# Projection stage of a two-layer graph network: query and key parts of four chunks per store, and value weights with the head index innermost

## The chip, the cores and the metric

The kernel runs on one core of a Trainium2 chip. The metric is the device time of one execution in microseconds (us); lower is better.

## The reference

A graph of 3327 nodes with 128 features, adjacency matrix `adj`, two layers. What matters here is layer 1:

```python
h = jnp.maximum(_layernorm(x), 0.0)
q = (h @ Wq.T).reshape(128, n, 8)      # 128 heads of the score matrix, 8 values for each node
k = (h @ Wk.T).reshape(128, n, 8)
v = (h @ Wv.T).reshape(128, n, 8)
a = softmax(einsum('dnh,dmh->dnm', q, k) * scale + adj + adj, axis=2)
x = x + einsum('dnm,dmh->dnh', a, v).reshape(n, 1024) @ Wo.T
```

The reshape is of memory as it lies, so one row of `h @ W.T` (1024 numbers for one node) is 128 groups t of 8 numbers h. The kernel calls t the token within a node and h the head index, and one scratch tensor in DRAM holds the 3328 x 128 = 425,984 tokens.

## The kernel before

The program is a row of stages, each closed by a barrier of all engines: a norm of the input, a stream over the adjacency matrix (layer 0), `finish_first_layer`, `project` (q, k and v of layer 1), `bound_scores`, a stage that is skipped when the bound is small, `split_shift`, the attention (by far the longest), and `project_out`. The change touches `finish_first_layer`, `project` and the scope of one tile.

**`finish_first_layer`** turns the weights on TensorE into PSUM (`y`), and ScalarE copies them to `w_t` (L432), columns in the order kind, h, t. ScalarE copies `wo_t` behind it (L433), and its next work is a square root (L435) that needs VectorE's variance.

**`project`** goes over C = 26 chunks. A chunk is 128 nodes, one for each partition (node p * 26 + c), so that each has a row of 1024 numbers for q, k and v. For each chunk:

- TensorE (L576) makes q, k, v in three PSUM tiles `pyq`, `pyk`, `pyv`, one of each, so the next chunk's q waits until VectorE and ScalarE have read this one's.
- ScalarE makes the bf16 first part (L591) and squares (L593) of q, then of k, then the second parts from `rest` (L596) of q, then of k.
- VectorE makes rest q (L612), the norm of q (L615), rest k (L612), the norm of k (L615), and then copies v from PSUM into `value[c % 2]` (L620). Ahead of that copy it waits for `value_stored[c % 2]`, that is until the values of chunk c - 2 have been stored from the same buffer (L619).
- GpSimd makes the third parts of q and of k (L558) and copies the next `h_now` (L550).
- SyncE issues all stores, in program order, on one queue. The values of every chunk go out as 128 rows of 4608 bytes (L528). The parts of q and k go out after every odd chunk (L525), six stores of two chunks: three parts of q, then three of k. SyncE waits for GpSimd's third part of q ahead of the first, and for that of k ahead of the fourth.

In DRAM a node's tokens of one head lie in one row, 128 bf16 numbers for each chunk, with neighbouring chunks side by side. Two chunks are a run of 512 bytes, so a store of one part is 128 partitions x 8 heads = 1024 runs. The tiles `parts` are double-buffered by pair (b = 0, 1), and ScalarE waits for `parts_stored` of the pair before last. After the chunks the two norm tensors (13,312 bytes for each partition) are stored, and the stage ends when everything has landed.

Of the kernel before, what the change touches and what calls it, by code (L numbers as in the profile page):

```python
# [18 lines left out]
ALU = mybir.AluOpType  # L19
ACT = mybir.ActivationFunctionType  # L20
F32 = mybir.dt.float32
BF16 = mybir.dt.bfloat16
# [346 lines left out]
def finish_first_layer(nc, w_in, w_out, wq, wk, wv, wo, keep):  # L369

    with ExitStack() as ctx:
# [57 lines left out]
        @block.scalar  # L429
        def _(act):  # L430
            act.wait_ge(w_turned, 1)
            act.activation(keep["w_t"][:], y[:, 0:6 * BANK], ACT.Copy)  # L432
            act.activation(keep["wo_t"][:].rearrange("p h o -> p (h o)"), y[:, 6 * BANK:8 * BANK], ACT.Copy).then_inc(w_kept, 1)  # L433
            act.wait_ge(variance_ready, 1)
            act.activation(stats[:, 2, :], stats[:, 1, :], ACT.Sqrt).then_inc(rooted, 1)  # L435
            act.wait_ge(h_turned, 1)
            act.activation(keep["h_t"][:, 4 * BANK:NP], y[:, 4 * BANK:NP], ACT.Copy)
# [34 lines left out]
def project(nc, qp_d, kp_d, v_d, nq_d, nk_d, keep):  # L472
# [4 lines left out]
    with ExitStack() as ctx:  # L477
        s = Scope(nc, ctx, "pr")
        W = H * P
        parts = [[s.sb(f"parts{kind}{b}", [P, PARTS, H, 2, P], BF16) for kind in "qk"] for b in range(2)]  # L480
        rest = [s.sb(f"rest{kind}", [P, W]) for kind in "qk"]
        squares = [s.sb(f"squares{kind}", [P, W]) for kind in "qk"]
        value = [s.sb(f"value{k}", [P, P, VW]) for k in range(2)]
# [8 lines left out]
        value_stored = [s.sem(f"value_stored{k}") for k in range(2)]  # L492
        block = ctx.enter_context(nc.Block())
        PS = 16 * PARTS
        assert C % 4 == 2

        def over_chunks(eng, do):

            with eng.Fori(0, C // 4) as i:
                for k in range(4):  # L500
                    do(i, k)
            for k in range(2):
                do(C // 4, k)

        def by_head(tile):
            return tile[:].rearrange("p (h t) -> p h t", h=H)
# [5 lines left out]
        @block.sync  # L512
        def _(sp):
            for k in range(2):
                for kind in range(2):
                    sp.sem_inc(parts_stored[k][kind], PS)
                sp.sem_inc(value_stored[k], 16)

            def store(i, k):
                c, b = 4 * i + k, k // 2  # L520
                if k % 2 == 1:
                    for kind, dst in enumerate((qp_d, kp_d)):
                        sp.wait_ge(part3[kind], c + 2)
                        for part in range(PARTS):
                            sp.dma_start(bass.AP(dst, part * H * TOK + (c - 1) * P, [[C * P, P], [TOK, H], [1, 2 * P]]),  # L525
                                         parts[b][kind][:, part].rearrange("p h c t -> p h (c t)")).then_inc(parts_stored[b][kind], 16)
                sp.wait_ge(value_kept, c + 2)
                sp.dma_start(bass.AP(v_d, c * (P * VW), [[C * P * VW, P], [1, P * VW]]),  # L528
                             value[k % 2][:].rearrange("p t v -> p (t v)")).then_inc(value_stored[k % 2], 16)

            over_chunks(sp, store)
            sp.wait_ge(rooted, 2)
            for kind, dst in enumerate((nq_d, nk_d)):
                sp.dma_start(bass.AP(dst, 0, [[C * P, P], [1, C * P]]), norm2[kind][:].rearrange("p c t -> p (c t)")).then_inc(norm_stored, 16)
            sp.wait_ge(norm_stored, 32)
            for b in range(2):
                pairs = (C // 2 + 1 - b) // 2
                for kind in range(2):
                    sp.wait_ge(parts_stored[b][kind], PS * pairs + PS)
                sp.wait_ge(value_stored[b], 16 * (C // 2) + 16)  # L540

        @block.gpsimd
        def _(pool):
            for kind in range(2):
                pool.sem_inc(part3[kind], 1)
            h_cols = keep["h_t"][:].rearrange("f (p j) -> f j p", j=C)

            def copy_h(c, k):
                pool.wait_ge(product[2], c + 1)
                pool.tensor_copy(h_now[k][:], h_cols[:, bass.ds(c, 1), :].rearrange("f o p -> f (o p)")).then_inc(h_copied, 1)  # L550

            def third_parts(i, k):
                c, b, half = 4 * i + k, k // 2, k % 2
                if not (isinstance(i, int) and c == C - 1):
                    copy_h(c + 1, 1 - half)
                for kind in range(2):
                    pool.wait_ge(part2[kind], c + 1)
                    pool.tensor_tensor(parts[b][kind][:, 2, :, half, :], by_head(rest[kind]), parts[b][kind][:, 1, :, half, :],  # L558
                                       ALU.subtract).then_inc(part3[kind], 1)

            copy_h(0, 0)
            over_chunks(pool, third_parts)

        @block.tensor
        def _(pe):
            def products(i, k):
                c = 4 * i + k
                pe.wait_ge(h_copied, c + 1)
                for kind in range(3):
                    if kind < 2:  # L570
                        pe.wait_ge(rest_left[kind], c + 1)
                        pe.wait_ge(squared[kind], c + 1)
                    else:
                        pe.wait_ge(value_kept, c + 1)
                    for b in range(0, W, BANK):
                        last = pe.matmul(py[kind][:, b:b + BANK], h_now[k % 2][:], keep["w_t"][:, kind * W + b:kind * W + b + BANK],  # L576
                                         start=True, stop=True)
                    last.then_inc(product[kind], 1)

            pe.sem_inc(product[2], 2)  # L580
            over_chunks(pe, products)

        @block.scalar
        def _(act):
            def copies(i, k):
                c, b, half = 4 * i + k, k // 2, k % 2
                for kind in range(2):
                    if half == 0:
                        act.wait_ge(parts_stored[b][kind], PS * i + PS)
                    act.wait_ge(product[kind], c + 1)  # L590
                    act.activation(parts[b][kind][:, 0, :, half, :], by_head(py[kind]), ACT.Copy, scale=(SCALE, 1.0)[kind])  # L591
                    act.wait_ge(summed[kind], c + 1)
                    act.activation(squares[kind][:], py[kind][:], ACT.Square).then_inc(squared[kind], 1)  # L593
                for kind in range(2):
                    act.wait_ge(rest_left[kind], c + 2)
                    act.activation(parts[b][kind][:, 1, :, half, :], by_head(rest[kind]), ACT.Copy).then_inc(part2[kind], 1)  # L596

            for kind in range(2):
                act.sem_inc(squared[kind], 1)
            over_chunks(act, copies)  # L600
            for kind in range(2):
                act.wait_ge(summed[kind], C + 1)
                act.activation(norm2[kind][:], norm2[kind][:], ACT.Sqrt, scale=(SCALE * SCALE, 1.0)[kind]).then_inc(rooted, 1)

        @block.vector
        def _(dve):
            def rests(i, k):
                c, b, half = 4 * i + k, k // 2, k % 2
                for kind in range(2):
                    dve.wait_ge(squared[kind], c + 2)  # L610
                    dve.wait_ge(part3[kind], c + 1)
                    dve.scalar_tensor_tensor(out=by_head(rest[kind]), in0=by_head(py[kind]), scalar=(SCALE, 1.0)[kind],  # L612
                                             in1=parts[b][kind][:, 0, :, half, :], op0=ALU.mult,
                                             op1=ALU.subtract).then_inc(rest_left[kind], 1)
                    dve.tensor_reduce(norm2[kind][:, bass.ds(c, 1), :].rearrange("p o t -> p (o t)"),  # L615
                                      squares[kind][:].rearrange("p (h t) -> p t h", h=H),
                                      AX_X, ALU.add).then_inc(summed[kind], 1)
                dve.wait_ge(product[2], c + 3)
                dve.wait_ge(value_stored[k % 2], 32 * i + (16 * b + 16))  # L619
                dve.tensor_copy(value[k % 2][:, :, 0:H].rearrange("p t h -> p h t"), by_head(py[2])).then_inc(value_kept, 1)  # L620

            dve.sem_inc(value_kept, 1)
            for k in range(2):
# [622 lines left out]
def gnn_two_layers(nc, x, adj, w_in, w_out, wq, wk, wv, wo, out):  # L1246
# [10 lines left out]
    with ExitStack() as ctx:  # L1257
# [3 lines left out]
        over = s.sb("over", [1, 1], I32)  # L1261
        with ExitStack() as early:
            e = Scope(nc, early, "early")
            keep |= {"h_nat": e.sb("h_nat", [P, C, F]), "w_t": e.sb("w_t", [P, 3 * H * P]), "h_t": e.sb("h_t", [P, NP])}
            with ExitStack() as layer:
                y = Scope(nc, layer, "layer1")
                keep |= {"h_int": y.sb("h_int", [P, C, F]), "in_acc": y.sb("in_acc", [P, NP]),
                         "out_acc": y.sb("out_acc", [P, NP]), "col_acc": y.sb("col_acc", [P, NP]),
                         "row_sum": y.sb("row_sum", [P, C])}
                load_and_norm_first(nc, x, keep)  # L1270
# [42 lines left out]
```

## Time and profile before

| | before |
|---|---|
| median of 3 runs | 10844.65 us (10841.93 to 10844.93) |
| profiled execution | 10844.98 us |
| its span in the profile | 10842.2 us |
| VectorE, ScalarE, TensorE, GpSimd busy | 89%, 94%, 96%, 77% |
| `finish_first_layer` | about 462 to 519 us |
| `project` | about 520 to 750 us |

The busy shares are those of the attention, which fills the span from about 810 to 10,720 us. The projection stage is 2% of the span and has limits of its own, so it has to be read by itself. The 2.8 us between the profiled time and its span lie outside the span; the profiled execution is 0.3 us above the median.

### The profile page before, as it was taken

How to read it: one execution, taken by the hardware profiler on the slowest of the kernel's cores; microseconds unless marked ns; L12 is line 12 of the kernel's file. 1: busy time of each engine (PE TensorE's matmuls, PEld its weight loads, DVE VectorE, ACT ScalarE, POOL GpSimd, SP SyncE). 2: the span in 40 equal slices, each digit the busy share in tenths (PEclk: the TensorE clock that was granted, in tenths of full speed). 3: DMA queues.
4: the chain of work that ended last, by engine and by line, in shares of the span. 5: the costliest groups of instructions: out<-in, count | busy, mean ns of one | idle time of the engine just before them, and what ended most of it. 6: DMA issues, size and time to landing. Idle time of an engine off the chain costs nothing. (4 is left out here: it accounts for less than half of the span.)

```text
span 10842.2 us, 542229 instructions
## 1 busy us (share of the span) xinstructions
PE 10388.2 (96%) x216535; PEld 6735.1 (62%) x216535; DVE 9621.0 (89%) x10382; ACT 10161.1 (94%) x7714; POOL 8392.4 (77%) x4260
## 2 busy tenths in 40 slices
PE   7749999999999999999999999999999999999998
PEld 6616666666666666666666666666666666666666
DVE  7688999999998999999998999999998999999997
ACT  4359999999999999999999999999999999999996
POOL 4347888888887888888887888888887888888885
PEclk9889999999999999999999999999999999999999
DMA  6582111111112111111112111111112111111113
GB/s 228 173 270 61 42 42 42 42 42 42 42 42 82 42 43 42 42 42 42 42 42 81 43 42 42 42 42 42 42 42 81 42 42 42 42 42 42 42 42 85
DMA packets 579449, 652.51 MB, mean 60 GB/s; under 512 B 172173, under 2 KB 517907, under 8 KB 573523
## 3 DMA queue, kind: packets, MB, share of 16 engines
q1 hardware_dynamic: 576786, 621.07, 20.5%
q8 instruction: 1799, 29.47, 1.1%
q0 software_dynamic: 832, 1.71, 0.0%
q14 instruction: 32, 0.26, 0.0%
HBM read 485.17 MB, written 137.18 MB: 57 GB/s over the span
## 5 line engine op out<-in xcount | busy, mean ns | idle before, releaser
L1084 DVE SCALAR_TENSOR_TENSOR at_sum<-attention_adj_t,at_score 128x832 f32<-128x832 f32 x9216 | 8805.5, 1017 | 961.2 <-PE at_score L1020 869.4
L1000 POOL TENSOR_TENSOR at_single<-at_single,attention_adj_t 128x832 f32<-128x832 f32 x4096 | 8056.1, 1989 | 1866.4 <-ACT at_single L1101 1827.6
L1020 PE MATMUL at_score<-at_q,at_k 128*32 128x512 bf16 (+1 forms) x106496 | 7213.9, 347 | 202.9 <-DVE at_sum L1084 148.0
L1104 ACT ACTIVATE at_sum<-at_sum 128x2496 f32<-128x2496 f32 x3072 | 7358.6, 2395 | 14.4 <-DVE at_sum L1084 14.3
L1020 PEld LDWEIGHTS at_score<-at_q,at_k 128*32 128x32 bf16 x106496 | 3572.7, 145 | 2368.9 <-DVE at_sum L1084 965.4
L1036 PE MATMUL at_acc<-at_sum,at_v 128*9 128x208 f32 x73728 | 4846.6, 339 | 3.4 <-issue 2.4
L1101 ACT ACTIVATE at_single<-at_score 128x832 f32<-128x832 f32 x4096 | 3718.3, 956 | 113.3 <-PE at_score L1020 112.9
L1036 PEld LDWEIGHTS at_acc<-at_sum,at_v 128*9 128x9 f32 x73728 | 1872.5, 91 | 906.7 <-issue 6.1
L1036 PE MATMUL at_acc<-at_single,at_v 128*9 128x208 f32 x32768 | 2155.4, 339 | 0.0
L1036 PEld LDWEIGHTS at_acc<-at_single,at_v 128*9 128x9 f32 x32768 | 833.0, 91 | 404.3 <-issue 1.5
L288 POOL TENSOR_TENSOR layer_col_acc<-layer_col_acc,st_a_rows 128x3328 f32<-128x3328 f32 x26 | 189.2, 7278 | 182.6 <-DMA st_a_rows<-in_adj_dram 182.6
L316 PEld LDWEIGHTS st_in_sum<-st_a_t,layer_h_int 128*128 128x128 f32 x1352 | 174.8, 192 | 67.2 <-issue 56.6
L336 ACT ACTIVATE st_a_t<-st_tp 128x512 f32<-128x512 f32 (+1 forms) x182 | 101.5, 564 | 106.2 <-PE st_tp L304 105.0
L359 DVE TENSOR_TENSOR layer_out_acc<-layer_out_acc,st_out_sum 128x512 f32<-128x512 f32 (+1 forms) x182 | 113.0, 645 | 93.4 <-PE st_out_sum L308 93.4
L1073 DVE COPY at_o<-at_acc 128x208 f32<-128x208 f32 x513 | 188.8, 368 | 5.0 <-PE at_acc L1036 5.0
L308 PE MATMUL st_out_sum<-st_a_rows,st_h_now 128*128 128x512 f32 (+1 forms) x364 | 178.3, 572 | 0.0
L316 PE MATMUL st_in_sum<-st_a_t,layer_h_int 128*128 128x128 f32 x1352 | 177.2, 276 | 0.0
L304 PE MATMUL st_tp<-all_ident,st_a_rows 128*128 128x128 f32 x676 | 108.6, 281 | 58.6 <-DMA st_a_rows<-in_adj_dram 58.6
L304 PEld LDWEIGHTS st_tp<-all_ident,st_a_rows 128*128 128x128 f32 x676 | 94.6, 196 | 72.6 <-issue 71.6
L334 ACT ACTIVATE st_e_t<-st_tp 128x256 f32<-128x256 f32 (+1 forms) x78 | 35.4, 454 | 99.8 <-PE st_tp L304 99.8
L558 POOL TENSOR_TENSOR pr_partsq<-pr_restq,pr_partsq 128x1024 bf16<-128x1024 f32 x26 | 55.4, 2129 | 68.5 <-ACT pr_partsq L596 68.5
L576 PE MATMUL pr_pyv<-early_w_t,pr_h_now 128*128 128x512 f32 x104 | 51.5, 617 | 44.4 <-DVE pr_value L620 44.4
(123 smaller groups left out, 1363.8 us busy)
## 6 DMA issues: line engine op xcount, KB each, us to landing
at_k<-k_parts_scratch SPq DMA_DIRECT2D x1536, 156.0 KB
at_q<-q_parts_scratch SPq DMA_DIRECT2D x4608, 13.0 KB
at_v<-v_scratch SPq DMA_DIRECT2D x512, 112.5 KB
adj_t_scratch<-st_a_t SPq DMA_DIRECT2D x26, 1664.0 KB, 7.6
st_a_rows<-in_adj_dram SPq DMA_DIRECT2D x25, 1663.5 KB, 9.2
attended_scratch<-at_o SPq DMA_DIRECT2D x1920, 7.3 KB
attention_adj_t<-adj_t_scratch SPq DMA_DIRECT2D x12, 2080.0 KB, 18.9
q_parts_scratch<-pr_partsq SPq DMA_DIRECT2D x39, 512.0 KB, 4.6
```

Of the source, the lines that this page charges most:

```text
L288: pool.tensor_tensor(keep["col_acc"][:], keep["col_acc"][:], a_rows[k][:], ALU.add).then_inc(pool_added, 1)
L304: last = pe.transpose(tp[(G * k + g) % 2][:, m * P:(m + 1) * P], a_cols[:, j, :], keep["ident"][:])
L308: pe.matmul(out_sum[(G * k + g) % 2][:, 0:b - a], h_now[k][:], a_rows[k][:, a:b], start=True, stop=True).then_inc(out_ready, 1)
L316: last = pe.matmul(in_sum[k][:, 0:P], keep["h_int"][:, j, :], a_t[k][:, j, :], start=(j == 0), stop=(j == C - 1))
L359: dve.tensor_tensor(keep["out_acc"][:, a:b], keep["out_acc"][:, a:b], out_sum[(G * k + g) % 2][:, 0:b - a], ALU.add).then_inc(out_added, 1)
L1000: pool.tensor_tensor(slot(n), slot(n), at[:, plan.chunk[n], :], ALU.mult).then_inc(multiplied, 1)
L1020: last = pe.matmul(score[plan.buffer(n)][32 * t:32 * (t + 1), a:b], keys[:, 32 * t:32 * (t + 1)], q[k][:, a:b], start=True, stop=True, til ...
L1036: last = pe.matmul(acc[k][32 * t:32 * t + VW, 0:QW], v[k][:, plan.chunk[n % STEPS], :], slot(n)[:, t * QW:(t + 1) * QW], start=(m % C == 0 ...
L1073: dve.tensor_copy(o[k][:], acc[k][:, 0:QW]).then_inc(kept, 1)
L1084: dve.scalar_tensor_tensor(out=slot(n), in0=at[:, plan.chunk[n], :], scalar=2.0, in1=score[plan.buffer(n)][:, 0:NB], op0=ALU.mult, op1=ALU ...
L1101: act.activation(slot(n), score[plan.buffer(n)][:, 0:NB], ACT.Exp).then_inc(exped, 1)
L1104: act.activation(sums[buffer][:], sums[buffer][:], ACT.Exp).then_inc(exped, 1)
```

## The change

`project` works on groups of eight chunks instead of four, with `parts` tiles for four chunks (RUN = 4) instead of two. The parts of q and k are stored after chunks 3, 7, 11, 15, 19 and 23, four chunks at a time in runs of 1024 bytes, and after chunk 25 the last two chunks, in runs of 512 bytes. The value weights in `w_t` are laid out with the head index innermost (ScalarE writes them with a stride), so `pyv` holds t, h and the copy to `value` reads and writes eight neighbouring numbers at a time; `value` has 9 columns for each t, the ninth being 1. The layout in DRAM is the same as before. The tile `h_nat` moves to a scope that is closed before `project`, which makes room for the larger tiles.

```diff
@@ finish_first_layer, ScalarE
-            act.activation(keep["w_t"][:], y[:, 0:6 * BANK], ACT.Copy)
+            act.activation(keep["w_t"][:, 0:4 * BANK], y[:, 0:4 * BANK], ACT.Copy)
+            act.activation(keep["w_t"][:, 4 * BANK:6 * BANK].rearrange("p (t h) -> p h t", h=H),
+                           y[:, 4 * BANK:6 * BANK].rearrange("p (h t) -> p h t", h=H), ACT.Copy)
@@ project
-        parts = [[s.sb(f"parts{kind}{b}", [P, PARTS, H, 2, P], BF16) for kind in "qk"] for b in range(2)]
+        RUN, AT_ONCE = 4, 8
+        parts = [[s.sb(f"parts{kind}{b}", [P, PARTS, H, RUN, P], BF16) for kind in "qk"] for b in range(2)]
...
             def store(i, k):
-                c, b = 4 * i + k, k // 2
-                if k % 2 == 1:
+                c, b = AT_ONCE * i + k, k // RUN
+                run = k % RUN + 1
+                if run == RUN or isinstance(i, int) and c == C - 1:
                     for kind, dst in enumerate((qp_d, kp_d)):
                         sp.wait_ge(part3[kind], c + 2)
                         for part in range(PARTS):
-                            sp.dma_start(bass.AP(dst, part * H * TOK + (c - 1) * P, [[C * P, P], [TOK, H], [1, 2 * P]]),
-                                         parts[b][kind][:, part].rearrange("p h c t -> p h (c t)")).then_inc(parts_stored[b][kind], 16)
+                            sp.dma_start(bass.AP(dst, part * H * TOK + (c + 1 - run) * P, [[C * P, P], [TOK, H], [1, run * P]]),
+                                         parts[b][kind][:, part, :, 0:run, :].rearrange("p h c t -> p h (c t)")).then_inc(parts_stored[b][kind], 16)
...
@@ project, ScalarE
-                    if half == 0:
+                    if place == 0:
                         act.wait_ge(parts_stored[b][kind], PS * i + PS)
...
@@ project, VectorE
-                dve.wait_ge(value_stored[k % 2], 32 * i + (16 * b + 16))
-                dve.tensor_copy(value[k % 2][:, :, 0:H].rearrange("p t h -> p h t"), by_head(py[2])).then_inc(value_kept, 1)
+                dve.wait_ge(value_stored[k % 2], 8 * AT_ONCE * i + (16 * (k // 2) + 16))
+                dve.tensor_copy(value[k % 2][:, :, 0:H], py[2][:].rearrange("p (t h) -> p t h", h=H)).then_inc(value_kept, 1)
```

On SyncE the order of issues in the projection loop of before is this, from the first chunk of a group of four (128x8x256 is a store of one part of two chunks):

```order
L528 ISA
L528 DMA v_scratch<-pr_value 128x1152
L523 REGISTER_ALU
L525 ISA
L525 DMA q_parts_scratch<-pr_partsq 128x8x256
L525 ISA
L525 DMA q_parts_scratch<-pr_partsq 128x8x256
L525 ISA
L525 DMA q_parts_scratch<-pr_partsq 128x8x256
L525 DMA k_parts_scratch<-pr_partsk 128x8x256 x3
L528 ISA
L528 DMA v_scratch<-pr_value 128x1152
```

After the change the same engine has this from the third chunk of a group of eight (128x8x512 is a store of one part of four chunks):

```order
L532 DMA v_scratch<-pr_value 128x1152
L527 REGISTER_ALU
L529 ISA
L529 DMA q_parts_scratch<-pr_partsq 128x8x512
L529 ISA
L529 DMA q_parts_scratch<-pr_partsq 128x8x512
L529 ISA
L529 DMA q_parts_scratch<-pr_partsq 128x8x512
L529 DMA k_parts_scratch<-pr_partsk 128x8x512 x3
L532 ISA
L532 DMA v_scratch<-pr_value 128x1152
```

The values of chunks 0, 1 and 2 of a group now go out with no parts ahead of them, and those of chunk 3 go out behind six stores of twice the size. On VectorE the order of instructions is unchanged.

## Rows read from the trace of the kernel before

**Rows 1.** Busy time by stretch: length, each engine, granted clock, DMA share, GB/s.

```profile
600.00:616.00 16.00, 11.82 (x26) 4.42 (x25) 16.00 (x11) 11.99 (x13) 9.26 (x6) 1.00 0.92 280
732.00:740.00 8.00, 0.00 (x0) 0.00 (x0) 0.00 (x0) 2.02 (x1) 0.00 (x0) 0.50 1.05 294
```

**Rows 2.** Timeline of VectorE in the projection: start us, us, instruction.

```profile
604.36 2.01 DVE L620 COPY pr_value<-pr_pyv 128x1024 f32<-128x1024 f32 x1
606.19 1.23 DVE L612 SCALAR_TENSOR_TENSOR pr_restq<-pr_pyq,pr_partsq 128x1024 f32<-128x1024 f32 x1
607.33 1.94 DVE L615 TENSOR_REDUCE pr_norm2q<-pr_squaresq 128x1024 f32 x1
609.16 1.23 DVE L612 SCALAR_TENSOR_TENSOR pr_restk<-pr_pyk,pr_partsk 128x1024 f32<-128x1024 f32 x1
610.29 1.95 DVE L615 TENSOR_REDUCE pr_norm2k<-pr_squaresk 128x1024 f32 x1
612.14 2.00 DVE L620 COPY pr_value<-pr_pyv 128x1024 f32<-128x1024 f32 x1
613.97 1.23 DVE L612 SCALAR_TENSOR_TENSOR pr_restq<-pr_pyq,pr_partsq 128x1024 f32<-128x1024 f32 x1
...
619.92 1.99 DVE L620 COPY pr_value<-pr_pyv 128x1024 f32<-128x1024 f32 x1
```

**Rows 3.** Timeline of SyncE's issues, same stretch.

```profile
603.12 2.41 SPq L525 DMA_DIRECT2D q_parts_scratch<-pr_partsq  x3
605.96 4.84 SPq L525 DMA_DIRECT2D k_parts_scratch<-pr_partsk  x3
611.00 3.65 SPq L528 DMA_DIRECT2D v_scratch<-pr_value  x2
```

**Rows 4.** DMA rate in 40 slices of 600.00 to 631.10 us, 0.78 us each.

```profile
GB/s 397 421 403 24 0 225 265 303 262 299 265 300 281 279 287 277 287 288 291 392 379 427 415 42 0 229 264 301 265 297 265 299 284 277 287 276 293 285 290 383
```

**Rows 5.** DMA of 603.9 to 614.5 us: packets, bytes, share.

```profile
DMA packets 5859, 2.96 MB, mean 279 GB/s; under 512 B 80, under 2 KB 5859, under 8 KB 5859
q1 hardware_dynamic: 5859, 2.96, 100.9%
```

**Rows 6.** DMA of 614.9 to 617.3 us, the value stores.

```profile
DMA packets 363, 0.98 MB, mean 407 GB/s; under 512 B 32, under 2 KB 166, under 8 KB 363
q1 hardware_dynamic: 363, 0.98, 105.2%
```

**Rows 7.** DMA of 741 to 749 us, the norm stores.

```profile
DMA packets 290, 3.41 MB, mean 426 GB/s; under 512 B 32, under 2 KB 32, under 8 KB 35
q1 hardware_dynamic: 290, 3.41, 100.8%
```

**Rows 8.** Value stores: time from issue to landing.

```profile
DMA to landing us min/median/max: 2.8/5.2/6.3
```

**Rows 9.** Timeline of VectorE and ScalarE between two chunks.

```profile
640.30 1.22 DVE L612 SCALAR_TENSOR_TENSOR pr_restk<-pr_pyk,pr_partsk 128x1024 f32<-128x1024 f32 x1
...
641.55 1.06 ACT L596 ACTIVATE pr_partsk<-pr_restk 128x1024 bf16<-128x1024 f32 x1 [1.92 <-DVE pr_restk L612]
...
642.51 1.01 ACT L591 ACTIVATE pr_partsq<-pr_pyq 128x1024 bf16<-128x1024 f32 x1
...
643.42 1.02 ACT L593 ACTIVATE pr_squaresq<-pr_pyq 128x1024 f32<-128x1024 f32 x1
```

**Rows 10.** Timeline at the end of the projection.

```profile
727.56 2.42 SPq L525 DMA_DIRECT2D q_parts_scratch<-pr_partsq  x3
...
738.45 1.21 SPq L534 DMA_DIRECT2D k_norm_scratch<-pr_norm2k  x1
...
750.07 0.06 DVE L670 MEMSET softmax_shift<- 128x1 f32 x1 [19.10 <-PEq L477]
```

**Rows 11.** Timeline of `finish_first_layer`, ScalarE and one VectorE copy.

```profile
493.94 2.73 ACT L432 ACTIVATE early_w_t<-fl_y 128x3072 f32<-128x3072 f32 x1 [54.61 <-PE fl_y L421]
...
506.71 0.23 ACT L435 ACTIVATE fl_stats<-fl_stats 128x26 f32<-128x26 f32 x1 [7.82 <-DVE fl_stats L84]
...
517.22 2.29 DVE L469 COPY early_h_t<-fl_y 128x2048 f32<-128x2048 f32 x1 [4.72 <-PE fl_y L426]
```

More of the change, by code:

```diff
@@ L494, in project @@
         PS = 16 * PARTS
-        assert C % 4 == 2
+        assert C % AT_ONCE == 2
         def over_chunks(eng, do):
-            with eng.Fori(0, C // 4) as i:
-                for k in range(4):
+            with eng.Fori(0, C // AT_ONCE) as i:
+                for k in range(AT_ONCE):
                     do(i, k)
             for k in range(2):
-                do(C // 4, k)
+                do(C // AT_ONCE, k)
         def by_head(tile):
@@ L536, in _ @@
             for b in range(2):
-                pairs = (C // 2 + 1 - b) // 2
+                runs = (-(-C // RUN) + 1 - b) // 2
                 for kind in range(2):
-                    sp.wait_ge(parts_stored[b][kind], PS * pairs + PS)
+                    sp.wait_ge(parts_stored[b][kind], PS * runs + PS)
                 sp.wait_ge(value_stored[b], 16 * (C // 2) + 16)
@@ L552, in third_parts @@
             def third_parts(i, k):
-                c, b, half = 4 * i + k, k // 2, k % 2
+                c, b, place = AT_ONCE * i + k, k // RUN, k % RUN
                 if not (isinstance(i, int) and c == C - 1):
-                    copy_h(c + 1, 1 - half)
+                    copy_h(c + 1, 1 - k % 2)
                 for kind in range(2):
                     pool.wait_ge(part2[kind], c + 1)
-                    pool.tensor_tensor(parts[b][kind][:, 2, :, half, :], by_head(rest[kind]), parts[b][kind][:, 1, :, half, :],
+                    pool.tensor_tensor(parts[b][kind][:, 2, :, place, :], by_head(rest[kind]), parts[b][kind][:, 1, :, place, :],
                                        ALU.subtract).then_inc(part3[kind], 1)
@@ L566, in products @@
             def products(i, k):
-                c = 4 * i + k
+                c = AT_ONCE * i + k
                 pe.wait_ge(h_copied, c + 1)
@@ L585, in copies @@
             def copies(i, k):
-                c, b, half = 4 * i + k, k // 2, k % 2
+                c, b, place = AT_ONCE * i + k, k // RUN, k % RUN
                 for kind in range(2):
-                    if half == 0:
+                    if place == 0:
                         act.wait_ge(parts_stored[b][kind], PS * i + PS)
                     act.wait_ge(product[kind], c + 1)
-                    act.activation(parts[b][kind][:, 0, :, half, :], by_head(py[kind]), ACT.Copy, scale=(SCALE, 1.0)[kind])
+                    act.activation(parts[b][kind][:, 0, :, place, :], by_head(py[kind]), ACT.Copy, scale=(SCALE, 1.0)[kind])
                     act.wait_ge(summed[kind], c + 1)
@@ L595, in copies @@
                     act.wait_ge(rest_left[kind], c + 2)
-                    act.activation(parts[b][kind][:, 1, :, half, :], by_head(rest[kind]), ACT.Copy).then_inc(part2[kind], 1)
+                    act.activation(parts[b][kind][:, 1, :, place, :], by_head(rest[kind]), ACT.Copy).then_inc(part2[kind], 1)
             for kind in range(2):
@@ L607, in rests @@
             def rests(i, k):
-                c, b, half = 4 * i + k, k // 2, k % 2
+                c, b, place = AT_ONCE * i + k, k // RUN, k % RUN
                 for kind in range(2):
@@ L612, in rests @@
                     dve.scalar_tensor_tensor(out=by_head(rest[kind]), in0=by_head(py[kind]), scalar=(SCALE, 1.0)[kind],
-                                             in1=parts[b][kind][:, 0, :, half, :], op0=ALU.mult,
+                                             in1=parts[b][kind][:, 0, :, place, :], op0=ALU.mult,
                                              op1=ALU.subtract).then_inc(rest_left[kind], 1)
@@ L1263, in gnn_two_layers @@
             e = Scope(nc, early, "early")
-            keep |= {"h_nat": e.sb("h_nat", [P, C, F]), "w_t": e.sb("w_t", [P, 3 * H * P]), "h_t": e.sb("h_t", [P, NP])}
+            keep |= {"w_t": e.sb("w_t", [P, 3 * H * P]), "h_t": e.sb("h_t", [P, NP])}
             with ExitStack() as layer:
                 y = Scope(nc, layer, "layer1")
-                keep |= {"h_int": y.sb("h_int", [P, C, F]), "in_acc": y.sb("in_acc", [P, NP]),
+                keep |= {"h_nat": y.sb("h_nat", [P, C, F]), "h_int": y.sb("h_int", [P, C, F]), "in_acc": y.sb("in_acc", [P, NP]),
                          "out_acc": y.sb("out_acc", [P, NP]), "col_acc": y.sb("col_acc", [P, NP]),
```

## The prediction

> **What bounds the kernel now.** I first looked at the busy time by stretch, since the page's shares are those of the attention, which the change leaves alone. In 16 us of the projection VectorE is busy for 16.00 us, TensorE for 11.82, ScalarE for 11.99, GpSimd for 9.26, and the DMA engines at 0.92 of their time [rows 1]. So VectorE sets the pace and the DMA engines come close behind it. After the last chunk VectorE has nothing to do while the DMA engines are full [rows 1]: there the DMA alone sets the end.
>
> The timeline of VectorE gives the pace. A record's length overlaps the next one, so I take start to start: rest q 1.14, norm q 1.83, rest k 1.13, norm k 1.85, value copy 1.83, sum 7.78 us for a chunk [rows 2].
>
> Then the DMA. In the strip of rates one pair of chunks reads as follows: nothing up to about 603.9 us, parts at some 280 GB/s up to 614.8, values at 380 to 427 GB/s for 3 us, nothing again [rows 4]. The parts were issued from 603.12 and the values of the same chunk from 611.00 [rows 3], yet these landed 5.2 us later (the median) [rows 8], at 616.2, when the strip shows the parts gone and one value store's bytes moved. So the queue is served in order: a value store waits for all parts issued ahead of it. Call the first issue of q's parts X. The values of that chunk (copied at 604.36 [rows 2], X + 1.2) land at X + 13.1, and the buffer is wanted again by the copy two chunks on, at 619.92 [rows 2], X + 16.8. The slack is 3.7 us. This is the cover to watch.
>
> **The change part by part.**
>
> *Value copy.* The copy of 1024 numbers takes 1.83 us with writes 36 bytes apart; rest k, also 1024 numbers out of PSUM but with neighbouring writes, takes 1.13 [rows 2], and a plain copy of 2048 takes 2.29, 1.15 for half of it [rows 11]. The new writes go eight neighbours at a time with a gap of one. Bounds: 1.13 and 1.83. I take 1.13, since nothing else than the neighbourhood distinguishes the old copy from rest k, so VectorE alone could do a chunk in 7.08 us. The trace has no copy with rows of eight. The Trainium skill (SBUF — State Buffer, the note on SBUF cachelines under its port map) has SBUF in 16-byte lines that want two accesses each for full speed, by which the new copy would lose the penalty; no row here shows the line itself.
>
> *The next limit on VectorE.* From the start of rest k at 640.30 ScalarE does second part k, first part q and squares q of the next chunk, to 643.42 + 1.02 = 644.44, 4.14 us later [rows 9], and rest q waits for that. From rest q to rest k are 1.14 + 1.83 = 2.97. Together with 0.04 for the semaphore a chunk can't be below 7.15 us. The gain is 7.78 - 7.15 = 0.63 us for each chunk, not 0.70.
>
> *Cost of a packet.* At 512 bytes: 10.6 us x 16 engines x 1.009 / 5859 = 29 ns [rows 5]. At 4608 bytes: of 363 packets 166 are small (134 of them of the parts), which leaves 197 in 2.4 x 16 x (1.0 to 1.05) - 134 x 0.029 = 34.5 to 36.4 us, some 180 ns [rows 6]. At 13,312 bytes: 8 x 16 x 1.008 / 258 = 500 ns [rows 7]. The first two give 29 + 0.037 ns for each byte above 512, the last two 0.037 as well, so a packet of 1024 bytes is put at 48 ns. Its bounds: 38 ns (nothing but bytes, at the 27 bytes a ns of the longest) and 58 (twice a short one).
>
> *The burst.* A group's parts are 6 stores x 1024 runs = 6144 packets, before as after; after, each is twice as long. They take B = 6144 x 48 / 16 = 18.4 us, where they took 6144 x 29 / 16 = 11.1. For four chunks that is 18.4 instead of 22.2, so the DMA work falls: with four value stores of 1.4 us it is 24 us against a VectorE time of 28.6. Yet it comes at once. The values of chunk 3 of the run land at X + 18.4 + 2.0 = X + 20.4 (2.0 is what before has beyond its 11.1). Their buffer is wanted by chunk 5's copy at X + 16.8 - 2 x 0.63 = X + 15.5. The slack of 3.7 turns into a **stall of 4.9 us** of VectorE at `value_stored`, once in four chunks. Behind it on VectorE stand rest q and k of chunk 6; TensorE waits for `pyv`, ScalarE for rest q and GpSimd for ScalarE, so the whole loop stands. Four chunks take 28.6 + 4.9 = 33.5 us instead of 31.1. Nothing is carried to the next burst, since the queue is empty again by then.
>
> *Up to the last big burst.* It starts in chunk 23. Ahead of it lie 23 value copies, 23 x 0.63 = 14.5 us gained, and the stalls behind the bursts of chunks 3, 7, 11, 15 and 19, 5 x 4.9 = 24.5 us lost: +10.0 us.
>
> *The tail.* Before, from the first issue for chunk 25 (727.56 [rows 10]) the DMA has 0.5 for the start, 11.1 of parts, 1.5 of values, 8.0 of norms (3.41 MB at 426 GB/s [rows 7]), 21.1 us, that is 748.7; the next stage starts at 750.07 [rows 10]. Counted from chunk 23 it is 2 x 7.78 more, 36.7. After, the queue is never empty from chunk 23 on: 0.5 + 18.4 + values of 23 and 24, 3.0, + last parts, still short packets, 11.1 + 1.5 + 8.0 = 42.5 us. The parts of 24 and 25 are ready at X + 14.3, when the queue is still full, and the sixth stall is hidden in this. **+5.8 us.**
>
> *At nothing.* The weight copy: one instruction of 2.73 us becomes one of two thirds and a strided one of one third, which at twice the time adds about 1 us; ScalarE then idles 7.82 us up to L435 [rows 11], which hides it (uncovered it would be 1 us). `h_nat`'s scope: no instruction. The waits for `parts_stored`: each buffer is wanted four chunks after its burst began, 33 us, and B is 18.4. Three loop turns instead of six: VectorE's starts show no gap.
>
> Sum against the profiled execution: -14.5 + 24.5 + 5.8 = +15.8, and 10844.98 + 15.8 = **10860.8 us**; the profile lies 0.3 us above the median of the runs, so 10860.6 is the number. In general, with the cheap copy, the change is 5 (B - 13.5) + (B - 12.6) - 14.5 us, that is 6 B - 94.6.
>
> **The rivals.**
>
> *R1, slower: long packets are no cheaper for each byte.* Place: the burst. At 58 ns B = 22.3, the stall 8.8, the sum 6 x 22.3 - 94.6 = +39, 10884 us. It decides (more than 0.2%) from B = 19.4, that is 50.5 ns a packet. For it: no row shows a store of 1024-byte runs, and HBM may have its own say in how fast separate runs are written. Against it: the three lengths seen lie on one line with 10 ns that each packet costs besides its bytes [rows 5 to 7]. The Trainium skill (DMA: Bandwidth & Descriptors, Specifications) lets transfers reach line rate from 512 bytes up, by which 1024 bytes would bring nothing over 512 and this rival would hold; this trace has 279 GB/s at 512 bytes and 407 to 426 at the longer ones, which speaks against the rule.
>
> *R2: the copy doesn't get cheaper* (rows of eight cost as much as the stride). The norms, which read rows of eight with a stride, take 1.83 to 1.85 too [rows 2], and can't say whether row or stride costs it. Then nothing is gained, chunk 5's copy comes at X + 16.8, the stall is 3.6: 5 x 3.6 + 5.8 = +23.8, 10869 us.
>
> *R3, the lowest: value stores don't wait behind the burst,* or it is so short that they needn't. For: the DMA work falls. Against: the landing of [rows 8] behind [rows 3]. Then -14.5 is all of the loop, and with the tail at +5.8 it is -8.7, 10836 us. With 38 ns a packet B is 14.6 and the sum -7, 10838.
>
> **How the numbers follow.** The forecast has 0.60, R1 0.15, R2 0.12, R3 0.10, and 0.03 is left for a gain that I can't place (all VectorE could give is 26 x 0.70 = 18.2 us). The range goes from R3's 10836 to just above R1's 10884; the forecast's own, 42 to 54 ns, is 10847 to 10875. About 0.2%, 21.7 us, is what a measurement of this kernel can tell from no change. The forecast is above it from 50.5 ns on, which I give 0.09 of its 0.60; R1's 0.15 is above it, and 0.07 of R2's. Slower 0.31, faster 0.03, the same 0.66.
>
> **What would show it.** In the profile after: value copies of about 1.2 to 1.3 us in place of 2.0, and starts 1.13 apart from the next where nothing waits; chunks 7.1 to 7.2 us apart inside a run; VectorE idle for some 5 us ahead of the value copies of chunks 5, 9, 13, 17, 21 and 25, released by the DMA of the values; 1024-byte packets at 48 ns, 340 GB/s in the strip; the DMA idle for about 9 us of each 33; the next stage 16 us later. I would be wrong if VectorE shows no such idle time, if it exceeds 7 us, or if something in the attention moves.

## The result, and the profile after

The changed kernel takes 10862.15 us (median of 20 runs, 10855.25 to 10874.71), the kernel before in the same comparison 10842.58 us (20 runs, 10835.88 to 10848.24). The ratio is 1.0019, 95% interval 1.0012 to 1.0026: 19.6 us slower, with an interval of 13 to 28 us. The forecast was 10860.6 us and +15.8.

The total hides two things of opposite sign. These lines of VectorE's timeline, with its idle time in brackets, show the projection inside a run of four chunks and across the wait that the prediction placed at chunk 9, and what comes behind it:

```profile
592.63 1.21 DVE L624 COPY pr_value<-pr_pyv 128x1024 f32<-128x1024 f32 x1
...
599.88 1.21 DVE L624 COPY pr_value<-pr_pyv 128x1024 f32<-128x1024 f32 x1
...
605.18 1.95 DVE L619 TENSOR_REDUCE pr_norm2k<-pr_squaresk 128x1024 f32 x1
613.22 1.22 DVE L624 COPY pr_value<-pr_pyv 128x1024 f32<-128x1024 f32 x1 [6.10 <-DMA v_scratch<-pr_value]
...
621.87 1.22 DVE L616 SCALAR_TENSOR_TENSOR pr_restq<-pr_pyq,pr_partsq 128x1024 f32<-128x1024 f32 x1 [0.34 <-ACT pr_squaresq L597]
...
627.85 1.22 DVE L624 COPY pr_value<-pr_pyv 128x1024 f32<-128x1024 f32 x1
...
635.00 1.22 DVE L624 COPY pr_value<-pr_pyv 128x1024 f32<-128x1024 f32 x1
...
648.42 1.23 DVE L624 COPY pr_value<-pr_pyv 128x1024 f32<-128x1024 f32 x1 [6.17 <-DMA v_scratch<-pr_value]
...
658.23 1.22 DVE L616 SCALAR_TENSOR_TENSOR pr_restq<-pr_pyq,pr_partsq 128x1024 f32<-128x1024 f32 x1 [1.54 <-ACT pr_squaresq L597]
```

The copy takes 1.21 us where [rows 2] had 2.00, and rest k and norms are as before. Chunks 11 and 12 (627.85 and 635.00) are 7.15 us apart; chunks 7 and 8, right behind a wait, 7.25. Once in four chunks VectorE stands for 6 us, released by the DMA of the values. Behind each of the first five stalls there is a second, short one, which the prediction doesn't have. Added up from 535 to 780 us (engine, what it waited for, us in total, times, longest):

```profile
DVE pr_value L624 <- DMA v_scratch<-pr_value: 37.9, 6, 7.1
DVE pr_restq L616 <- ACT pr_squaresq L597: 5.3, 5, 1.6
```

SyncE's issues give the length of a group of four chunks and the tail:

```profile
591.77 2.48 SPq L529 DMA_DIRECT2D q_parts_scratch<-pr_partsq  x3
...
603.70 18.32 SPq L532 DMA_DIRECT2D v_scratch<-pr_value  x4
626.98 2.46 SPq L529 DMA_DIRECT2D q_parts_scratch<-pr_partsq  x3
...
734.99 2.48 SPq L529 DMA_DIRECT2D q_parts_scratch<-pr_partsq  x3
...
778.84 0.32 SPq L661 DMA_DIRECT2D bo_nk<-k_norm_scratch  x1
```

From the burst at 591.77 to the next are 35.2 us. Over all five gaps between the six big bursts it is 35.2 to 37.2 and 36.1 on the mean (31.1 before, 33.5 forecast). From the last big burst to the next stage are 43.85. The queue's packets, 593 to 610 us, in the middle of a burst, answer to [rows 5]:

```profile
DMA packets 5743, 5.80 MB, mean 341 GB/s; under 512 B 80, under 2 KB 5743, under 8 KB 5743
q1 hardware_dynamic: 5743, 5.80, 103.9%
```

A packet of 1024 bytes takes 17 us x 16 engines / 5743 = 47 ns if the engines are taken as full (49 with the share of 103.9% that the line shows); 48 were forecast. The rate is 341 GB/s against 279.

The next stage begins with this row, which answers to the last of [rows 10]:

```profile
778.90 0.06 DVE L674 MEMSET softmax_shift<- 128x1 f32 x1 [21.18 <-PEq L479]
```

So the projection ends 28.8 us later than before (750.07), yet the profiled executions differ by 17.0 us (10862.02 against 10844.98). The other 12 come back in the attention, a stage with not one edited line. Both the loss and the gain needed an explanation by experiment.

### The profile page after: what moved, and what is told of

It reads as the page before. It is cut to its first block and busy times, and to the rows that moved or that the text cites. A ratio compares the mean times of both kernels' runs of the same rounds, so it can differ in the third digit from the quotient of the medians.

```text
span 10860.0 us, 542092 instructions
## 1 busy us (share of the span) xinstructions
PE 10393.5 (96%) x216535; PEld 6736.4 (62%) x216535; DVE 9604.3 (88%) x10382; ACT 10159.6 (94%) x7715; POOL 8394.2 (77%) x4260
```

## The experiments

Times are medians beside those of the kernel before from the same chip; the edits are shown in excerpts. "Next stage" is the start of the memset of `softmax_shift`.

**Copy alone.** Before, with the new weight layout (ScalarE's two copies, not shown again) and copy:

```diff
...
-dve.tensor_copy(value[k % 2][:, :, 0:H].rearrange("p t h -> p h t"), by_head(py[2])).then_inc(value_kept, 1)
+dve.tensor_copy(value[k % 2][:, :, 0:H], py[2][:].rearrange("p (t h) -> p t h", h=H)).then_inc(value_kept, 1)
```

> Before, with the new weight layout and value copy alone; parts stored by pairs as before. Theory (the loss of the change comes from its bursts alone, the copy is a gain): chunks about 7.15 us apart, values landing 14.1 us after the first issue of q's parts and wanted at 15.5, so no stall; the next stage starts 25 x 0.63 = 15.7 us earlier than before, near 734 us, total some 16 us under before. Rival (the DMA becomes the limit once VectorE is faster: 14.1 us of DMA in 14.3 for a pair): waits of about 1 us ahead of value copies and a gain under 10 us. The attention's own time is expected unchanged by both.

Measured: 10824.8 us against 10838.8, ratio 0.9987 (0.9978 to 0.9996). The start of the next stage:

```profile
736.00 0.06 DVE L672 MEMSET softmax_shift<- 128x1 f32 x1 [20.38 <-PEq L479]
```

That is 14.1 us earlier, where 15.7 were expected; the loop began 0.9 us late (first rest q at 529.22 us, at 528.29 in before). VectorE never waited for a value store. Pairs came 14.3 us apart, and the DMA was at 102% of its time from 600 to 628 us:

```profile
q1 hardware_dynamic: 12945, 8.58, 102.4%
```

The copy is the gain of the change and needs no longer runs. The rival was not far off: VectorE and the DMA are now level. The attention, expected unchanged, was 7 us shorter (see the table below), and the total still gave 14.0 us for 16 expected.

**Runs alone.** The change, with the old layout (ScalarE's part not shown) and copy.

```diff
...
-dve.tensor_copy(value[k % 2][:, :, 0:H], py[2][:].rearrange("p (t h) -> p t h", h=H)).then_inc(value_kept, 1)
+dve.tensor_copy(value[k % 2][:, :, 0:H].rearrange("p t h -> p h t"), by_head(py[2])).then_inc(value_kept, 1)
```

> The change without the new weight layout and value copy: four chunks for a store, copy with its stride. Theory: the stall moves with the landing (21.4 us after the first issue of q's parts) against a later need (16.8), 4.6 us at six value copies, 23 us before the last burst, some 2 us of late restarts, tail +5.9: next stage +30 us against before. Rival (the stall's size is set by something other than that landing, a fixed cost for each burst of 6 us as after the change): next stage +38 us or more.

Measured: 10865.6 us against 10838.8, ratio 1.0025 (1.0015 to 1.0035).

```profile
DVE pr_value L622 <- DMA v_scratch<-pr_value: 29.4, 6, 5.1
DVE pr_restq L614 <- ACT pr_squaresq L595: 2.9, 4, 1.1
```

The stall is 4.9 us on the mean instead of 6.3: it shrinks because VectorE arrives later, which excludes a fixed cost for each burst. The next stage came at 787.57, +37.5, where I had +30. Of this, 2.9 us were there before the loop (its first rest q ran at 531.22 us, at 528.29 in before), 24.3 are five stalls, 2.9 the late restarts and 6.0 the tail; 1.4 are not placed. The total alone would have spoken for the rival; the wait itself does not.

**Values first.** The change, with each chunk's value store issued ahead of its parts.

```diff
 def store(i, k):
     c, b = AT_ONCE * i + k, k // RUN
     run = k % RUN + 1
+    sp.wait_ge(value_kept, c + 2)
+    sp.dma_start(..., value[k % 2][:] ...).then_inc(value_stored[k % 2], 16)
     if run == RUN or isinstance(i, int) and c == C - 1:
         ...
-    sp.wait_ge(value_kept, c + 2)
-    sp.dma_start(..., value[k % 2][:] ...).then_inc(value_stored[k % 2], 16)
```

> The change with each chunk's value store issued ahead of its parts. Theory (the stall is the value store queued behind the burst): values of chunk 3 of a run land at once and the stalls of 6 us at chunks 5, 9, 13 ... vanish; the burst starts 3 us later, the values of the next chunk are now behind it, landing 24.4 us after q's parts are ready and wanted at 22.7, so stalls of about 1.7 us at chunks 6, 10, 14 ...; tail +7: next stage about +1 us against before (+29 for the change). Rival (the burst itself slows or holds the other engines or stores, wherever values stand in the queue): stalls of 5 us or more remain and the next stage stays above +20.

Measured: 10842.3 us against 10838.8, ratio 1.0004 (0.9995 to 1.0013); next stage at 758.65, +8.6.

```profile
DVE pr_value L624 <- DMA v_scratch<-pr_value: 11.0, 5, 3.0
DVE pr_restq L616 <- ACT pr_squaresq L597: 3.0, 4, 1.7
```

The six waits of 6 us are gone, and five of 1 to 3 us stand one chunk later, behind the next value store that is queued after the burst. The place is as the theory says. The next stage was expected near +1, and of the 7.6 us beyond that the stalls are 2.5 (2.2 us each on the mean where I had 1.7), the late restarts, again not in my sum, are 3.0, and the loop began 0.7 late (528.96); 1.4 are not placed. The rival needed more than +20.

**Four value buffers.** The change with the order of stores left alone, and four each of `value` and `value_stored`.

```diff
-value = [s.sb(f"value{k}", [P, P, VW]) for k in range(2)]
+value = [s.sb(f"value{k}", [P, P, VW]) for k in range(4)]
...
-dve.wait_ge(value_stored[k % 2], 8 * AT_ONCE * i + (16 * (k // 2) + 16))
+dve.wait_ge(value_stored[k % 4], 4 * AT_ONCE * i + (16 * (k // 4) + 16))
```

> The change with four value buffers instead of two; order of stores and bursts as in the change. Theory (VectorE stood only because it wanted a value buffer whose store was behind the burst): the value copy of chunk 5 now wants the buffer of chunk 1, long stored; no stalls, no late restarts, chunks 7.15 us apart, and only the tail of +5.9 is left: next stage near 741 us against 750 for before and 779 for the change. Rival (the burst slows the engines' own accesses or the whole loop): chunks well over 7.2 us apart during bursts, next stage over 755.

Measured: 10835.6 us against 10836.5, ratio 0.9999 (0.9990 to 1.0008). VectorE had no wait left in the loop, neither the long nor the short one. Its value copies run on through the burst that was issued from 614.54:

```profile
615.41 1.22 DVE L626 COPY pr_value<-pr_pyv 128x1024 f32<-128x1024 f32 x1
...
622.56 1.22 DVE L626 COPY pr_value<-pr_pyv 128x1024 f32<-128x1024 f32 x1
...
629.71 1.21 DVE L626 COPY pr_value<-pr_pyv 128x1024 f32<-128x1024 f32 x1
```

They are 7.15 us apart. The next stage came at 744.40, 5.7 us before that of before, in a program that had begun the loop 2.4 us late (530.65 against 528.29): 8.0 net, where 9 were expected. This is the experiment that shows the cause: same bursts, same order, more buffers, no stall. It also shows what bursts cost where nothing stands behind them: 744.40 against 736.00 with pairs, with 1.4 of the 8.4 already there at the loop's start (530.65 against 529.22). The other 7.0 are the tail: from the issue of chunk 23's parts to the next stage it is 43.9 us here (from 700.46) and 36.7 with pairs (from 699.29).

**Loops for eight chunks alone.** Before, with `AT_ONCE = 8` and `RUN = 2`: the same work and the same stores by pairs, in a longer program. Every engine's projection loop is longer, and `h_nat` keeps the scope that it has in the change. In short:

```diff
-with eng.Fori(0, C // 4) as i:
-    for k in range(4):
+with eng.Fori(0, C // 8) as i:
+    for k in range(8):
         do(i, k)
```

> Before, with only the projection's loops written for eight chunks a turn (stores by pairs, old copy, old layout). It asks where 12 us of the attention went between the two profiles, 9899.6 to 9887.6 us from its first to its last copy of a head. Theory A (that is chance from run to run): total equal to before within 0.1%, the attention anywhere in 9885 to 9900. Theory B (more instructions ahead of the attention shift how its code is fetched): the attention again near 9888 and the total some 9 us under before. Projection stage: unchanged, next stage within 1 us of before.

Measured: 10833.5 us against 10838.8, ratio 0.9995 (0.9986 to 1.0004); next stage at 750.83. The ratio doesn't decide, and nor does the attention's whole length: 9892.9 us fits chance, which allowed 9885 to 9900, better than the 9888 of theory B. Its parts say more. I took the starts of VectorE's 513 copies of `at_acc` from each trace (one for each head and a last one). The attention runs through four blocks of 128 heads; TensorE and ScalarE have one loop for all of them, VectorE, GpSimd and SyncE a loop for each block. In the third block four heads take half a microsecond less in this kernel, as in the changed one.

**VectorE's loop for eight chunks alone.** Before, with the edit above for VectorE's projection loop only.

> Before, with VectorE's loop of the projection alone written for eight chunks a turn; nothing else differs. In the attention's third block of heads a group of four heads takes 76.5 us in all four kernels whose projection is written for eight chunks and 77.0 in the two written for four. VectorE is the engine with a loop of its own for each block. Theory B (the place of VectorE's code): third block again 76.5, total 4 to 6 us under before. Rival (another engine's code, or chance): third block 77.0, total equal to before.

The expectation calls VectorE the engine with a loop for each block; by the program GpSimd and SyncE have one too, but this edit leaves theirs alone.

Measured: 10827.6 us against 10836.5, ratio 0.9991 (0.9982 to 1.0000), 8.9 us less where 4 to 6 were expected. The third block is short again (76.50). The waits of ScalarE in 6200 to 7700 us, inside that block, were in before

```profile
ACT at_single L1101 <- PE at_score L1020: 10.1, 19, 0.9
```

and with the edit

```profile
ACT at_single L1101 <- PE at_score L1020: 2.6, 4, 1.0
```

The same wait in the same 1500 us is 9.3 to 10.2 us in the four traces with the long third block and 2.3 to 4.9 in the seven with the short one.

**Both kernels once more,** unchanged, one execution each, profiled.

> The kernel before, profiled a second time, to see how far the attention's length moves by itself. Theory (part of the 12 us by which the two first profiles' attentions differ is chance, part is the third block): the third block again 77.0 us for four heads, the whole attention some 6 us below the 9899.6 us of the first profile; next stage after the projection at 750 within 1 us. Rival (all 12 us belong to the kernels): 9899 to 9901 again.

> The changed kernel, profiled a second time. Theory: six waits for the value store of 6 to 7 us again, next stage at 779 within 2 us, third block 76.5 us for four heads, attention 9884 to 9892. Rival (the stalls or the short third block were chance): next stage off by more than 3 us, or third block at 77.0.

Measured: before 10841.9 us, next stage at 750.48; the change 10860.6 us, next stage at 778.52, with the stalls of the first profile:

```profile
DVE pr_value L624 <- DMA v_scratch<-pr_value: 38.0, 6, 7.1
DVE pr_restq L616 <- ACT pr_squaresq L597: 3.9, 5, 1.5
```

The attention of before came out at 9896.5, 3 us below the first profile and not the 6 that I had expected. All traces together (first to last copy of `at_acc`; four heads is the median of start to start over four heads inside the third block):

```
kernel                       attention us   four heads, third block   next stage
before                       9899.6         77.00                     750.07
before again                 9896.5         77.01                     750.48
copy alone                   9892.6         77.02                     736.00
four value buffers           9892.7         76.98                     744.40
change                       9887.6         76.48                     778.90
change again                 9887.1         76.50                     778.52
runs alone                   9890.9         76.48                     787.57
values first                 9884.1         76.63                     758.65
loops for eight chunks       9892.9         76.49                     750.83
VectorE for eight chunks     9887.9         76.50                     749.22
copy, loops for eight        9889.4         76.48                     736.41
```

The third block has two levels, 77.0 and about 76.5 (76.63 in one trace), and for each of the two kernels profiled twice both profiles fall on the same one. As a whole the block took 2476.6 to 2479.6 us in the first four traces and 2467.6 to 2472.2 in the other seven, while the other three blocks show no such split. The attention's whole length scatters too much to tell the two groups apart (9892.6 to 9899.6 against 9884.1 to 9892.9). It isn't the loop of eight by itself, since the kernel with four value buffers has it too and sits at 77.0; that one has two more instructions on VectorE ahead of its projection loop and other waits in it. So an edit to VectorE's code in an earlier stage is enough to shorten the third block, by 4 to 12 us between any two traces. How, is open. That the place of the third loop's code decides it is what I take it for, but no run moved the code and nothing else. The DMA queues that load instructions don't tell the two levels apart: from 6200 to 7700 us before has 273 such packets and the kernel with VectorE's edit 274, all on one queue.

**Copy, and loops for eight chunks.** The fastest combination that the runs pointed to.

> The fastest combination that the first runs point to: stores by pairs, the new weight layout and value copy, loops written for eight chunks. Theory: next stage near 736 as with the copy alone, third block of the attention 76.5 us for four heads; total some 19 us under before (14 of the projection, 5 of the attention). Rival (code placement was chance): total like the copy alone, 14 us under before.

Measured: 10814.9 us against 10836.5, ratio 0.9979 (0.9970 to 0.9988), next stage at 736.41, third block 76.48. It beats both kernels: it is 21.7 us under before, and 13.7 of that are there when the next stage starts. The rest comes behind the projection, and since its cause is open it may go with the next edit.

## Why the prediction was right in its total, and where it was not

*Right by the runs.* The mechanism: a faster copy, a burst that delays the value store behind it, a stall at the value copies of chunks 5, 9, 13, 17, 21 and 25, and a longer tail. The copy and the next limit: value copies are 7.15 us apart where nothing waits, as forecast, and 1.21 us long. The 1024-byte packet: 47 to 49 ns against 48. The tail: 43.85 us from the last big burst (734.99) to SyncE's first issue of the next stage (778.84), against 37.9 in before, from this row to 750.00:

```profile
712.12 2.54 SPq L525 DMA_DIRECT2D q_parts_scratch<-pr_partsq  x3
```

That is +6.0 for +5.8. Both lengths are 1.2 to 1.4 us above my sums (42.5 and 36.7), and the difference cancels this. The terms at nothing held: the strided third of the weight copy took 2.01 us, ScalarE's idle time ahead of the root was 6.83 us instead of 7.82, and the first rest q came at 528.06 us, at 528.29 in before. R1 (long packets no cheaper) and R2 (copy no cheaper) are excluded by these rows, R3 by the stalls. The rule of the Trainium skill (DMA: Bandwidth & Descriptors, Specifications) that 512 bytes are enough for line rate, by which R1 would have held, does not agree with these traces: 279 GB/s at 512 bytes, 341 at 1024.

*Mis-sized: the stall.* Forecast 4.9 us, measured 6.1 to 6.3 and once 7.1, which is over the 7 us that I had named as a sign of being wrong. The step that failed is the landing of the values at "5.2 us later (the median)". That median is over all value stores, and only every second one stands behind parts. The store issued at 611.00 us in before, asked for by itself, gives this:

```profile
DMA to landing us min/median/max: 6.2/6.2/6.2
```

It landed at 617.2, X + 14.1 and not X + 13.1, so before had 2.7 us of slack and not 3.7, and the constant behind B is 3.0. With it the stall comes out at 18.4 + 3.0 - 15.5 = 5.9; in the trace the values landed at X + 21.4 and VectorE came for the buffer at X + 15.3 (591.77 to 607.12). For the five stalls ahead of the last burst I had 24.5 us; they are 37.9 - 6.3 = 31.6. The first of them is 1 us longer than the others in both profiles of the change, because its values landed 10.2 us after their issue and the others' 9.3 to 9.5; why, is open.

*Missing: the restart.* "TensorE waits for `pyv`" was written down, and not what follows from it. TensorE's order is q, k, v, so while v of chunk 6 waits for the buffer, q of chunk 7 waits behind it. After the stall v, q and ScalarE's two reads of q must pass before rest q of chunk 7. By this timeline of the change they don't make it (it is behind the stall at chunk 13, with v of chunk 14 and q of chunk 15):

```profile
649.70 3.78 PE L580 MATMUL pr_pyv<-early_w_t,pr_h_now 128*128 128x512 f32 x4 [7.28 <-DVE pr_value L624]
...
653.27 2.95 PE L580 MATMUL pr_pyq<-early_w_t,pr_h_now 128*128 128x512 f32 x4
...
656.26 1.02 ACT L595 ACTIVATE pr_partsq<-pr_pyq 128x1024 bf16<-128x1024 f32 x1 [1.43 <-PE pr_pyq L580]
```

The four matmuls of v take 3.78 us instead of the 1.98 that they take in before, and those of q 2.95. After the stall at 613.22 (chunk 9) TensorE was faster again by the time it came to q, and VectorE's second wait was only 0.34 us:

```profile
614.50 3.65 PE L580 MATMUL pr_pyv<-early_w_t,pr_h_now 128*128 128x512 f32 x4 [7.20 <-DVE pr_value L624]
...
617.98 1.88 PE L580 MATMUL pr_pyq<-early_w_t,pr_h_now 128*128 128x512 f32 x4
```

The five cases split in this way: where q took 1.88 us the wait was 0.34 and 0.40 us, where it took 2.85 to 2.98 the wait was 1.44 to 1.57. With v at 1.98 and q at 1.88 rest q of chunk 7 would have come at most some 0.1 us late (an estimate from these rows). So the restart is late because TensorE comes back slow, which the last section shows. This costs 5.3 us ahead of the last burst, and it goes where the stall goes, as the four buffers show. Together: -14.5 + 31.6 + 5.3 = +22.4 up to the last burst, where the trace has 734.99 - 712.12 = +22.9 and I had +10.0; with the tail +28.8.

*Missed: the attention.* "If something in the attention moves" stood only among what would prove me wrong, and it did move. It gave back 12.0 us between the first two profiles and 9.4 between the second two. So +15.8 came near +19.6 because a loss undersized by 13 us met a gain of 9 to 12 that I had not seen. The forecast was good for the mechanism and partly lucky for the number.

## What to carry to other kernels

Longer runs for a store lowered the DMA's work here (1024 bytes in 47 ns instead of twice 29) and kept its queue busy with one burst for some 18 us instead of 11. What must be checked is the small store queued behind such a burst, and who wants its buffer and when. Take the landing of that very store, not the median of its group. And where a change of a few tens of us in one stage is compared by total time, look at the untouched stages too: here the attention moved by 9 to 12 us beside a change of 19.6.

## What the runs showed of the hardware that was not expected

TensorE, idle for 7 us at each stall, came back at the lower of its two clocks. The stretches of the change from 605 us show it (length, each engine, granted clock, DMA share, GB/s):

```profile
605.00:614.00 9.00, 1.99 (x4) 0.68 (x4) 2.90 (x3) 4.71 (x5) 3.49 (x3) 0.84 1.04 368
617.00:622.00 5.00, 5.00 (x11) 1.97 (x10) 4.66 (x5) 3.16 (x4) 4.17 (x3) 0.91 0.00 0
649.00:653.00 4.00, 3.30 (x4) 1.50 (x5) 4.00 (x4) 1.06 (x1) 1.06 (x1) 0.50 0.42 166
653.00:658.00 5.00, 5.00 (x10) 2.14 (x9) 3.70 (x3) 2.79 (x3) 3.56 (x3) 0.76 0.07 28
```

A granted clock of 0.50 is 1.2 GHz, and the four matmuls that take 1.98 us at 2.4 GHz took 3.78. A value between 0.50 and 1.00 is the mean of a stretch that has both levels in it. So each stall on VectorE cost more than its length here, by 0.3 to 1.6 us. The other surprise is the third block of the attention, 77.0 or 76.5 us for four heads, which changed with VectorE's code in an earlier stage and was the same in both profiles of each of the two kernels profiled twice; its mechanism is open.
